# Six images' second expert products inside the second attention, the last image's first two between the others' third ones

## The reference, cut to what matters

```
t = t + attention(layernorm(t))        # second attention: 64 heads of dimension 2, causal
x = layernorm(t)
feat = mean over the 8 images of x;  w = softmax(feat @ Wr + br)          # a weight for each token and expert
h = relu(bn1(x @ W1[e] + b1[e]))       # first product,  for each of 8 experts e
h = relu(bn2(h @ W2[e] + b2[e]))       # second product
y = h @ Wo[e] + bo[e]                  # third product
t = t + sum over e of y * w[:, e]
```

## Time and profile before

| | before |
|---|---|
| median of 3 runs | 3240.01 us (3239.32 to 3244.25) |
| profiled execution: its own time | 3235.75 us |
| its span, first to last instruction | 3234.0 us |
| PE busy, share of the span | 3021.5 us, 93% |
| ACT busy | 2709.7 us, 84% |
| DVE busy | 2003.0 us, 62% |
| mean granted TensorE clock | 0.989 |
| second attention, first to last exponential starts | 869.1 to 2950.9 us |
| thirds of images 0 to 5 and 7 | 3026.0 to 3230.8 us |

### The profile page before, as it was taken

How to read it: one execution, slowest core, us unless ns; L and a number is a source line. 1 busy time by engine, 2 the same in 40 slices (tenths; PEclk the granted TensorE clock), 3 DMA queues, 4 the chain that set the end, 5 groups by cost and what they waited for, 6 DMA issues and landing times.

```text
span 3234.0 us, 67658 instructions
## 1 busy us (share of the span) xinstructions
PE 3021.5 (93%) x27633; PEld 1006.2 (31%) x27633; DVE 2003.0 (62%) x2942; ACT 2709.7 (84%) x2580; POOL 265.7 (8%) x352
## 2 busy tenths in 40 slices
PE   6999999999798898999999999999999999899999
PEld 3455555544221122222222222222222222123444
DVE  5799999998656356456546646645655654343543
ACT  5555555554599999999999999999999999997586
POOL 7000000000210010010101001001001000000000
PEclk9999999999799999999999999999999999999999
DMA  6222202220100210211211211121121121111451
GB/s 217 75 55 57 53 22 54 57 54 10 56 25 18 62 28 18 62 41 34 78 44 34 68 53 34 34 78 44 34 78 44 34 78 44 45 34 51 176 170 45
DMA packets 153904, 185.93 MB, mean 57 GB/s; under 512 B 30870, under 2 KB 114932, under 8 KB 150524
## 3 DMA queue, kind: packets, MB, share of 16 engines
q1 hardware_dynamic: 152592, 180.79, 18.9%
q10 hardware_dynamic: 1004, 0.83, 0.1%
HBM read 95.48 MB, written 76.58 MB: 53 GB/s over the span
## 4 chain that ended last, share of the span: by engine, by line
PE 60%; ACT 21%; issue 9%; DVE 8%; DMA 1%; SPq 1%; POOL 0%; ACTq 0%; DVEq 0%
ACT arena L1053 21%; PE ps L1418 19%; PE ps L1371 8%; PE ps L1477 3%; PE ps L1136 3%; PE ps L1187 3%; PE ps L1484 3%; PE ps L1214 3%; PE ps L1437 3%; PE ps L1189 3%; PE ps L1198 3%; PE ps L1165 2%; DVE arena L1592 2%; DVE arena L1855 2%; DVE arena L1604 2%
## 5 line engine op out<-in xcount | busy, mean ns | idle before, releaser
L1053 ACT ACTIVATE arena<-ps 128x1536 f32<-128x1536 f32 x1536 | 2069.9, 1680 | 14.3 <-PE ps L1371 11.4
L1418 PE MATMUL ps<-arena 128*6 128x512 f32 (+4 forms) x12288 | 1209.2, 488 | 2.4 <-DVE arena L1872 2.4
L1872 DVE TENSOR_TENSOR arena<-arena,causal 128x512 f32<-128x512 f32 x1024 | 652.3, 684 | 215.7 <-ACT arena L1053 215.5
L1371 PE MATMUL ps<-arena 15*128 15x512 bf16 (+3 forms) x6144 | 603.7, 329 | 99.8 <-ACT arena L1053 97.3
L1371 PEld LDWEIGHTS ps<-arena 15*128 15x128 bf16 x6144 | 163.0, 91 | 1094.6 <-ACT arena L1053 827.1
L989 ACT ACTIVATE arena<-ps 128x512 f32<-128x512 f32 x512 | 300.8, 596 | 234.7 <-PE ps L1189 222.3
L1592 DVE TENSOR_REDUCE arena<-ps 128x32 bf16<-128x1024 f32 x256 | 310.3, 1214 | 64.4 <-PE ps L1165 64.3
L1599 DVE TENSOR_TENSOR arena<-arena,ps 128x512 f32<-128x512 f32 x512 | 328.7, 678 | 29.0 <-PE ps L1198 28.9
L1418 PEld LDWEIGHTS ps<-arena 128*6 128x6 f32 (+1 forms) x12288 | 216.0, 87 | 398.6 <-issue 318.2
L1187 PE MATMUL ps<-arena 96*128 96x256 bf16 x1024 | 257.1, 276 | 0.7 <-ACT arena L962 0.5
L1189 PE MATMUL ps<-arena 128*128 128x256 bf16 x1024 | 256.0, 275 | 0.0
(11 more groups left out here) (204 smaller groups left out, 2036.2 us busy)
## 6 DMA issues: line engine op xcount, KB each, us to landing
hidden<-arena SPq DMA_DIRECT2D x96, 256.0 KB, 2.4
arena<-hidden SPq DMA_DIRECT2D x24, 1024.0 KB, 5.3
arena<-qstack SPq DMA_DIRECT2D x512, 30.0 KB
parts<-arena SPq DMA_DIRECT2D x8, 1536.0 KB, 6.4
arena<-parts SPq DMA_DIRECT2D x48, 256.0 KB, 5.6
arena<-parts SPq DMA_DIRECT2D x96, 128.0 KB, 4.3
arena<-kstack SPq DMA_DIRECT2D x512, 24.0 KB
qstack<-arena SPq DMA_DIRECT2D x24, 384.0 KB, 3.3
```

Of the source, the lines that this page charges most:

```text
L1053: act.activation(PR1[:, at:at + CW], bank(BPC * (f % 2), BPC), ACT.Exp).then_inc(d_exp, 1)
L1371: mm = pe.matmul(bank(at + k)[:, s * P:(s + n) * P], Ks[par][HR * h:HR * h + QROWS, j * P:(j + 1) * P], Qs[par][HR * h:HR * h + QROWS, t * ...
L1418: mm = pe.matmul(o[HR * h:HR * h + m, :], V1[n % 2][:, j, v:v + m], PR1[:, at[h] + s * P:at[h] + (s + k) * P], start=q == 0, stop=(q, t + ...
L1872: dve.tensor_tensor(v, v, m3, ALU.min).then_inc(d_mask, 1)
```

## The change

1. A new slot 3, in step k = 11 of each group from image 2 on, holds kind "G": the second product of the same unit whose first product was slot 0. VectorE now turns the first product into `hidden1` with one instruction, max(A1*x, -B1), which is the relu without its shift B1; the shift's part of the second product is the same for every token and is put into the second relu's bias (B2x), made once by the new kind "K" (group 23). The second product is copied to `hidden2` (one buffer) and stored. The first product itself is not stored any more.
2. At the end, images 0 to 5 have only `relu2_loaded` (ACT, out of the loaded buffer), the weighting and the third.
3. The firsts and seconds of the last image are put between those thirds: in each six units one first (at the first unit) and one second (at the fourth); ScalarE does their relus after its second and its fifth. The results wait in sixteen buffers h2_last. The last image then has only weightings and thirds.
4. W2 is loaded with W1 early in the attention. SP stores the new product after it has issued the loads of group g+2, not before.

```
-MISC = (1, 5, 9)
+MISC = (1, 5, 9, 11)
...
-    if slot == 0:
-        return ("H", n - 2, gi) if n >= 2 else None
+    if slot in (0, 3):
+        if n >= 2:
+            return "HG"[slot // 3], n - 2, gi
+        return ("K", 0, 0) if (n, gi, slot) == (1, 7, 0) else None
...
+                elif kind == "G":
+                    pe.wait_ge(h_dve, n * GPI + name + 1)
+                    pe.matmul(o, W2[:, name % NE, :], hidden1, start=True, stop=True).then_inc(hg_pe, 1)
+                elif kind == "K":
+                    pe.wait_ge(w12_loaded, 2 * INC)
+                    pe.wait_ge(k_dve, 1)
+                    for e in range(NE):
+                        mm = pe.matmul(o[:, e * VC:(e + 1) * VC], W2[:, e, :], cv(c_B1 + e).to_broadcast([P, VC]),
+                                       start=True, stop=True)
+                    mm.then_inc(k_pe, 1)
...
                 if kind == "H":
+                    u, e = n * GPI + name, name % NE
+                    dve.wait_ge(h_pe, u + 1)
+                    wait(dve, hg_pe, u)
+                    dve.tensor_scalar(hidden1, o, cv(c_A1 + e), cv(c_nB1 + e), ALU.mult, ALU.max).then_inc(h_dve, 1)
+                elif kind == "G":
                     u = n * GPI + name
-                    dve.wait_ge(h_pe, u + 1)
-                    wait(dve, h_stored[u % STAGED], u // STAGED * INC)
-                    dve.tensor_copy(staged[u % STAGED], o).then_inc(h_dve, 1)
+                    dve.wait_ge(hg_pe, u + 1)
+                    wait(dve, h_stored, u * INC)
+                    dve.tensor_copy(hidden2, o).then_inc(hg_dve, 1)
...
+                    if q == NQ - 1:
+                        between(g, 3)
...
+            def relu2_loaded(p, k):
                 n, e = p * (2 * NE) + k, k % NE
+                act.wait_ge(h_loaded[k // KP], p * INC)
+                if n >= 2 * NE + 2:
+                    act.wait_ge(g_w, n - 1)
+                act.activation(h2[k % 2], pieces[k // KP][:, k % KP, :], ACT.Relu, bias=cv(c_B2x + e),
+                               scale=cv(c_A2 + e)).then_inc(g_r2, 1)
...
+            act.wait_ge(k_dve, 3)
+            for n in range(2 * NE, (B - 1) * 2 * NE):
+                relu2_loaded(n // (2 * NE), n % (2 * NE))
+                last, part = divmod(n - 2 * NE, NH)
+                if part == 1:
+                    relu1(1, last)
+                elif part == 4:
+                    relu2(1, last, h2_last[last], g_last)
...
-            for n in range(2 * NE + 2, (B - 1) * 2 * NE):
-                second(n // (2 * NE), n % (2 * NE))
-                third((n - 2) // (2 * NE), (n - 2) % (2 * NE))
...
+            for n in range(2 * NE, B * 2 * NE):
+                if n < (B - 1) * 2 * NE:
+                    last, part = divmod(n - 2 * NE, NH)
+                    if part == 0:
+                        first(1, last)
+                    elif part == 3:
+                        second(1, last)
+                third(n // (2 * NE), n % (2 * NE))
```

More of the change, by code:

```diff
@@ L280, in hybrid_kernel @@
         PR1 = cut([PRING * CW])
-        W1 = cut([NE, P])
+        W1, W2 = [cut([NE, P]) for _ in range(2)]
         in_h = cut.at
-        staged = [cut([HALF]) for _ in range(STAGED)]
+        hidden1, hidden2 = [cut([HALF]) for _ in range(2)]
         in_v = cut.at
@@ L323, in hybrid_kernel @@
         cut = Cut(in_h)
-        bias_w, wT = [cut([T]) for _ in range(2)]
+        bias_w = cut([T])
         cut = Cut()
@@ L330, in hybrid_kernel @@
         pieces = [cut([KP, HALF]) for _ in range(PIECES // 2)]
-        W2, Wo = [cut([NE, P]) for _ in range(2)]
+        wT = cut([T])
+        Wo = cut([NE, P])
         cut = Cut()
@@ L340, in hybrid_kernel @@
         h2 = [cut([HALF]) for _ in range(2)]
+        h2_last = [cut([HALF]) for _ in range(8)] + h2_first[10:] + h2_first[8:10]
         ps = ctx.enter_context(nc.psum_tensor("ps", [P, 8 * HALF], F32))
@@ L501, in all_stored @@
         def all_stored(eng):
-            for k in range(STAGED):
-                eng.wait_ge(h_stored[k], NH * GPI // STAGED * INC)
+            eng.wait_ge(h_stored, NH * GPI * INC)
         def hi_plane(k):
@@ L703, in _ @@
                 if n == B - 1 and gi == 3:
[L704 to L705 removed]
+                    sp.dma_start(Wo, a["L1_ffn_Wo"].rearrange("e d h -> d e h")).then_inc(ffn_w_loaded, INC)
+                if n >= 2:
+                    sp.wait_ge(hg_dve, (n - 2) * GPI + gi + 1)
+                    sp.dma_start(hidden[n - 2, gi // KP, :, gi % KP, :], hidden2).then_inc(h_stored, INC)
                 store_group(g, g % 2)
@@ L1053, in _, with relu1, relu2 @@
                 act.activation(PR1[:, at:at + CW], bank(BPC * (f % 2), BPC), ACT.Exp).then_inc(d_exp, 1)
-            def relu1(p, k):
-                n, e = p * (2 * NE) + k, k % NE
[L1058 to L1070, removed]
+            def relu1(m, k):
+                n, e = m * (2 * NE) + k, k % NE
+                act.wait_ge(g_h1, n + 1)
+                wait(act, g_h2, n - 1)
+                act.activation(h1[k % 2], bank(k % 2), ACT.Relu, bias=cv(c_B1 + e), scale=cv(c_A1 + e)).then_inc(g_r1, 1)
+            def relu2(m, k, to, made):
+                e = k % NE
+                act.wait_ge(g_h2, m * (2 * NE) + k + 1)
+                act.activation(to, bank(2 + k % 2), ACT.Relu, bias=cv(c_B2 + e), scale=cv(c_A2 + e)).then_inc(made, 1)
+            def relu2_loaded(p, k):
+                n, e = p * (2 * NE) + k, k % NE
+                act.wait_ge(h_loaded[k // KP], p * INC)
[3 more added lines that the diff above has]
+                               scale=cv(c_A2 + e)).then_inc(g_r2, 1)
             for k in range(2 * NE):
@@ L1077, in _ @@
                 if k:
[L1078 to L1088, removed]
+                    relu2(0, k - 1, h2_first[k - 1], g_r2)
+            relu2(0, 2 * NE - 1, h2_first[2 * NE - 1], g_r2)
+            act.wait_ge(k_dve, 3)
[6 more added lines that the diff above has]
+                    relu2(1, last, h2_last[last], g_last)
         @block.tensor
@@ L1466, in _, with first, second @@
             pe.wait_ge(ffn_w_loaded, FFN_LOADS * INC)
-            def first(p, k):
-                wait(pe, g_r1, p * (2 * NE) + k - 1)
-                pe.matmul(bank(k % 2), W1[:, k % NE, :], half(Yall[:, ORDER[p], :], k // NE), start=True, stop=True)\
+            def first(m, k):
+                wait(pe, g_r1, m * (2 * NE) + k - 1)
+                pe.matmul(bank(k % 2), W1[:, k % NE, :], half(Yall[:, B - 2 + m, :], k // NE), start=True, stop=True)\
                     .then_inc(g_h1, 1)
[L1473 to L1476, removed]
+            def second(m, k):
+                pe.wait_ge(g_r1, m * (2 * NE) + k + 1)
+                wait(pe, g_last if m else g_r2, k - 1)
                 pe.matmul(bank(2 + k % 2), W2[:, k % NE, :], h1[k % 2], start=True, stop=True).then_inc(g_h2, 1)
@@ L1943, in _ @@
                     n, th, e = p * (2 * NE) + k, k // NE, k % NE
-                    dve.wait_ge(g_r2, n + 1)
+                    if p < B - 1:
+                        dve.wait_ge(g_r2, n + 1)
+                    else:
+                        dve.wait_ge(g_last, k + 1)
                     dve.wait_ge(g_y3, n - 1)
-                    dve.tensor_tensor(h2w[k % 2], h2[k % 2], half(wB[:, e, :], th), ALU.mult).then_inc(g_w, 1)
+                    dve.tensor_tensor(h2w[k % 2], h2[k % 2] if p < B - 1 else h2_last[k], half(wB[:, e, :], th), ALU.mult).then_inc(g_w, 1)
                     if k == 0 and p > 1:
```

47 lines of the change are left out of this document (19 added, 28 removed).

## The result

| | before | after |
|---|---|---|
| median | 3240.36 us (4 runs, 3239.32 to 3244.25) | 3283.74 us (4 runs, 3281.06 to 3289.41) |
| ratio | | 1.0134, 95% interval 1.0116 to 1.0152 |
| span of the profiled execution | 3234.0 us | 3280.2 us (its own time 3281.95) |
| start of the last exponential | 2950.9 | 3048.7 |
| first third of images 0 to 5 | 3026.0 | 3124.5 |

The kernel became 1.3% slower, 43 us by the medians, where +51 was forecast. The profiled spans differ by 46.2 us: +97.8 up to the last exponential (95.9 of it in images 2 to 7, 0.7 in image 1, 1.2 ahead of the attention), +0.7 from there to the first third of image 0, -52.3 from there to the end.

A forecast was written before the change was run, and what follows sets the result against it. TensorE was taken to bound both attention and end; +98 us in the attention and -47 at the end gave +51, so 3287 us profiled and 3291 median. The forecast spanned 3279 to 3308 (67%), the stated range 3254 to 3306.

The forecast's parts named there:

- TensorE bounds both stretches: Attention and end: TensorE, not ScalarE, is the bound, so the change carries TensorE work from one into the other.
- the sign: Whole kernel: slower, given 89%; faster by more than 0.2% had 9%, within 0.2% had 2%.
- The rival that the attention takes the seconds into idle time: Attention: G fits into TensorE's 14.0 us idle an image, so the kernel ends at 3211 us; chance 8%.
- G at 1.06: Attention, step 11: each G costs 1.06 us, as H does behind a quad of values, not the end's 0.86.
- The groups: Attention, H to H: full groups go from 16.38 to 17.44 us, those with a free slot from 16.00 to 17.0.
- The room: Attention: TensorE may fall 0.66 to 0.83 us behind ScalarE before ScalarE stands; a free-slot group then loses 1.0.
- Covers in the attention: Attention: G's copy, single hidden2 buffer, later stores and wait for slot 2 (4 us of cover) are hidden, costing nothing.
- The rival of a new wait there: Attention: VectorE reads slot 2 late and G stands, 1 us in five groups of five images, 3315 us; chance 10%.
- The end: Thirds of images 0 to 5 and last image: 204.8 us become 158, saving 47, with 35 to 53 as range.
- The ring: End, images 0 to 5: first or second, relu, relu2_loaded, weighting and third wait in turn, 4.44 us per three units.
- The rival by which TensorE never waits: End: it runs at TensorE's work, 110 + 16 = 126 us, saving 79, net +19, 3259 us; chance 15%.
- The last image: End: weighting and third alone, through two buffers, take 0.99 us a unit, 16 us for its 16 units.

The follow-up runs named there:

- two edits: Changed kernel with the last image's relus and second product placed later and a third h2w buffer: 3258.91 us, ratio 1.0060 to the kernel before.
- the relus: Changed kernel with the last image's first relu, second product and second relu placed later among the thirds: 3266.82 us, ratio 1.0092 to the kernel before.

## Why the prediction was right

**TensorE bounds both stretches** of the kernel before: that held, and with it the sign. The idle time of TensorE in images 2 to 6 stayed at 70 us while 80 products were added, and taking G's columns away gave back 68.0 us for 68 of its own time. The rival that the attention takes the seconds into idle time falls with that; I had 8% on it. What failed in it is that it counts idle time over a whole stretch: the idle time lay before H and around the free steps 5 and 9.

**G at 1.06** was exact: all 96 cost that, none the 0.86 of the end. The price was taken over from a place that is not quite the same, though: in the earlier trace rows H follows the scores and a wait, while G follows a quad of values. That the two cost the same was not known before.

**The groups**: 17.44 and 17.0 forecast, 17.43 to 17.53 and 17.06 measured; 17 of the free ones had 16.12 before, so they lost 0.94. 98 us forecast, 95.9 measured: 54.8 in the full groups (55 forecast) and 41.1 in the others (43). Of the 2 us that are missing, 1.6 come from one event. In the profiled execution of the kernel before one group of image 7 took 17.71 us where its like take 16.12, and in it TensorE's granted clock was 0.55 for 4 us, which is near the lower of its two levels (1.2 of 2.4 GHz):
```profile
2788.10:2791.90 3.80, 3.80 (x24) 0.37 (x21) 1.58 (x3) 3.55 (x3) 0.00 (x0) 0.55 0.20 50
```
TensorE had stood 1.04 us for ScalarE just before, as in other groups in which the clock stays at 1.00; why it fell there is not shown. The changed kernel's attention has no such fall.

**The room** by which TensorE may fall behind ScalarE was mis-sized, 0.66 to 0.83 where about 0.6 was measured. The prediction's own sum gives 1.68 - 1.06 = 0.62, and ScalarE's rows give 1.03 - 0.43 = 0.60, since 0.43 of G's 1.03 reached it. The lower end of 0.66 left out that two ordinary steps ahead of H gain 0.03 each: in the earlier trace rows TensorE goes from 1810.50 to 1815.36 + 1.06 = 1816.42 in four steps, 5.92 - 4 x 1.333 = 0.59 behind. So H alone used the room up already in the kernel before. In a group that had lasted 16.00, whatever was put in step 11 was charged in full: 1.06 with all columns and 0.34 with 32. The forecast of 1.0 for such a group came this near because the room was set 0.1 too large only.

**Covers in the attention**: VectorE's added copy, the single buffer, the later store and the wait for slot 2 cost nothing that can be seen; the loss is G's own time, with 512 columns and with 32. VectorE's new instruction on H took 0.80 us, not the 0.69 of the old copy, without effect in step 1; in step 2 the same instruction was what the masks waited behind. The rival of a new wait there did not happen in the change, but did in an experiment.

**The end**: 47 us saved were forecast, 52.5 measured (204.8 to 152.3), at the edge of the 35 to 53 given. The ring was there as described, with 4.28 instead of 4.44 us a round. Two of its terms were mis-sized: ScalarE starts 1.06 after a first, not 1.12, and the third that waited costs 0.97, not 1.06. The rival by which TensorE never waits was the stretch of 109.8 us, which needed two edits to come within 2 us of (111.5). The last image took 16.6 us, 16 forecast.

So the sum was +51 with errors of -2 and -5.5, which makes +43.4. The spans have +46.2, because 1.9 us came on ahead of image 2 and 0.7 between the last exponential and the first third of image 0, which the sum had at nothing. The medians have +43. Of the 1.9, 1.2 lie ahead of the attention and can't be told from noise: in the traces of the eleven experiments the first exponential starts anywhere from 866.5 to 872.9 us.

**Where I erred was in the experiments.** For H in step 2 I took the catching up in step 1 as free. It isn't: TensorE can only catch up until it meets ScalarE (0.33 of waiting there), and what VectorE had queued behind H moved with it. For the relus I named one ring and overlooked the second, although its row stood among those I had read.

**What stays open.** In image 1, before the first H, the only added work is K, in group 23. That group takes 17.39 us instead of 16.07, and the next four take 15.96 to 16.03 instead of 16.12, so that 0.7 us of the loss remain. The kernel before too has groups of 15.97 at the start of the attention and of 16.12 later. Why a group without H takes now the one, now the other was not tried.

## What to carry to other kernels

An idle share of an engine in a stretch is no room for a further instruction. Ask at which step the idle time lies, what it waits for, and how far the engine may fall behind its partner before the partner stands (here about 0.6 us, with scores made two chunks ahead, and H had used it up). A product of 1.06 us was free in step 5 of a group with two free slots and cost 1.06 in step 11 of the same group. When work is interleaved into a queue, follow the ring that it closes through every engine's order of instructions, and when one ring is opened look for the next shorter one: here neither edit alone reached the work of the engine, both together did.

## What the hardware showed beyond that

The same float32 product of 128x512 costs TensorE 0.86 us in a stream of its like, 0.97 when it had to wait for its moving values and another like it follows, and 1.06 between the small matmuls of the attention, of which only 0.34 is left with 32 columns. ScalarE could use the result of a first or a second 1.06 us after its start, where it was waiting for it at the end, and 1.12 after a second in the earlier trace rows.
